# When the second group's rows are normalized and stored, and where four pieces of a column sum are added

## The reference, cut to what matters

```
def _gn(v):                       # 32 groups of one channel: mean and variance over the image
    return (v - mean) / sqrt(var + 1e-5)

x1  = x + L0(_gn(x))              # L0: 16 Fourier modes along rows, 16 along columns, plus a 1x1 mix
out = x1 + L1(_gn(x1))            # L1: deformable 3x3 convolution (offsets and mask from a 3x3 convolution)
```

## Time and profile before

| engine | busy us | share of the span |
|---|---|---|
| TensorE matmuls | 1690.6 | 95% |
| TensorE weight loads (beside matmuls) | 1326.2 | 75% |
| VectorE | 1317.5 | 74% |
| ScalarE | 1171.7 | 66% |
| GpSimd | 927.1 | 52% |

### The profile page before, as it was taken

The page is one execution under the profiler, slowest core; times in us unless marked ns, Lnnn a source line. Parts: engine busy times, 40 slices in busy tenths (PEclk is TensorE's granted clock), DMA queues, the critical chain, the costliest instruction groups (busy, mean ns, idle before and its releaser), DMA issues.

```text
span 1775.6 us, 159736 instructions
## 1 busy us (share of the span) xinstructions
PE 1690.6 (95%) x70973; PEld 1326.2 (75%) x70973; DVE 1317.5 (74%) x1964; ACT 1171.7 (66%) x1969; POOL 927.1 (52%) x1185
## 2 busy tenths in 40 slices
PE   8894579999999999999999999999999999999996
PEld 3542358888888888888888888888888888888885
DVE  7495447777777777777777777777777777777773
ACT  7175236677667676777676767776676767776773
POOL 0052335555556555655565555555565556555551
PEclk9796679999999999999999999999999999999998
DMA  9167554333333333333333333333333333333331
GB/s 383 34 252 282 178 175 123 92 85 95 99 97 84 91 99 99 86 89 97 99 89 88 90 99 96 84 92 99 98 85 90 97 99 88 88 97 99 90 89 31
DMA packets 162530, 196.58 MB, mean 111 GB/s; under 512 B 20384, under 2 KB 137536, under 8 KB 158400
## 3 DMA queue, kind: packets, MB, share of 16 engines
q1 hardware_dynamic: 162496, 196.17, 37.6%
HBM read 143.88 MB, written 52.22 MB: 110 GB/s over the span
## 4 chain that ended last, share of the span: by engine, by line
PE 91%; DMA 3%; DVE 2%; issue 1%; ACT 1%; POOL 0%; SPq 0%; DVEq 0%; POOLq 0%; ACTq 0%
PE pE L1131 18%; PE pVV L1211 16%; PE pE L1152 13%; PE pM L1177 10%; PE pVV L1152 9%; PE pVV L1165 7%; PE pR L1165 7%; PE pM L1187 4%; PE pE L1044 3%; DMA xh_scratch<-stg 1%; DMA win<-xh_scratch 1%; PE pE L1101 1%; DVE stg L846 0%; PE pVV L1079 0%; ACT stg L622 0%
## 5 line engine op out<-in xcount | busy, mean ns | idle before, releaser
L533 POOL COPY big<-win 128x480 f32<-128x480 f32 x520 | 291.7, 591 | 659.4 <-PE pVV L1165 439.6
L521 POOL TENSOR_TENSOR prod<-big 128x600 f32<-128x600 f32 (+1 forms) x489 | 499.5, 1043 | 30.0 <-POOL big L576 29.8
L666 ACT ACTIVATE big<-pE 128x768 f32<-128x768 f32 x390 | 334.3, 857 | 178.6 <-PE pE L1131 178.6
L882 DVE COPY big<-pE 128x768 f32<-128x768 f32 x390 | 373.0, 956 | 95.2 <-PE pE L1131 82.5
L888 DVE STREAM_TRANSPOSE big<-prod 128x768 f32<-128x768 f32 x390 | 377.7, 968 | 29.0 <-POOL prod L521 29.0
L1131 PE MATMUL pE<-big,sel_s 32*64 32x192 f32 x12480 | 356.9, 336 | 10.2 <-DVE big L882 7.8
L1131 PEld LDWEIGHTS pE<-big,sel_s 32*64 32x64 f32 x12480 | 219.3, 132 | 113.5 <-issue 60.7
L1211 PE MATMUL pVV<-big,wc 64*32 64x128 f32 x18720 | 293.7, 272 | 2.9 <-issue 2.0
L1211 PEld LDWEIGHTS pVV<-big,wc 64*32 64x32 f32 x18720 | 261.5, 106 | 44.4 <-issue 44.4
L1152 PE MATMUL pE<-big 60*32 60x72 f32 x20800 | 250.6, 232 | 4.5 <-issue 4.5
L1152 PEld LDWEIGHTS pE<-big 60*32 60x32 f32 x20800 | 230.6, 105 | 11.1 <-issue 5.1
(11 more groups left out here) (105 smaller groups left out, 1699.5 us busy)
## 6 DMA issues: line engine op xcount, KB each, us to landing
big<-xh_scratch SPq DMA_DIRECT2D x396, 136.0 KB
win<-xh_scratch SPq DMA_DIRECT2D x130, 408.0 KB, 3.7
xh_scratch<-stg SPq DMA_DIRECT2D x32, 544.0 KB, 2.9
big<-in_x SPq DMA_DIRECT2D x16, 1024.0 KB, 15.8
x_scratch<-big SPq DMA_DIRECT2D x16, 1024.0 KB, 4.7
x1r<-x_scratch SPq DMA_DIRECT2D x256, 64.0 KB, 3.0
out<-outs SPq DMA_DIRECT2D x256, 64.0 KB, 2.1
xh_scratch<-zero SPq DMA_DIRECT2D x4, 204.0 KB, 2.6
```

Source lines behind the costliest of these rows:

```text
L521: made = nc.gpsimd.tensor_tensor(prod[:, kx, at:at + m, 0:SQ].rearrange("p m (a b) -> p m a b", a=NSH), hy.to_broadcast(shape), hx.to_broa ...
L533: last = nc.gpsimd.tensor_copy(strips[:, half * HTP:(half + 1) * HTP, h, 0:REG].rearrange("p t (r x) -> p t r x", r=WIN_R), tiles_of(q, h, ...
L666: nc.scalar.activation(*expanded(kx, 0), ACT.Copy).then_inc(e_read, 1)
L882: nc.vector.tensor_copy(*expanded(kx, 1)).then_inc(e_read, 1)
```

## The change

Two things change. First, LATE and LATE_X1: the sixteen restores of group 1 go, one each, to the ends of VectorE's steps 1 to 16, their stores to SP's steps 2 to 17, and the eight x1 stores to SP's steps 1, 3, ..., 15. The three restores ahead of the steps are gone. The written-out part of VectorE's and SP's programs reaches to step 18 instead of 4. Second, in the first stage GpSimd adds the first two chunks of each piece of x (`pairs`, two buffers), and TensorE multiplies the other two chunks and that sum by the identity, three chunks a piece where there were four; a further semaphore (`pair_read`) tells GpSimd that a buffer has been read.

```diff
-LATE_X1 = {-3: (0,), -2: (1,), -1: (2,), 0: (3,), 1: (4,), 2: (5,), 3: (6,), 4: (7,)}
+LATE_STEPS = 16
+LATE_X1 = {2 * i + 1: (i,) for i in range(LOADS)}
-LATE = {-4: range(0, 3), -3: range(3, 6), -2: range(6, 9), -1: range(9, 12), 0: range(12, 14), 1: range(14, 16)}
+LATE = {k + 1: (k,) for k in range(LATE_STEPS)}
...
+        pairs = [big[:, HW + i * XCH:HW + (i + 1) * XCH] for i in range(2)]
...
-                peeled(at, g * NSET + 5 if apart else start)
-                at = looped(g * NSET + 5 if apart else start, (g + 1) * NSET - 3 if apart else end, g)
+                head = g * NSET + (5 if g else LATE_STEPS + 3)
+                peeled(at, head if apart else start)
+                at = looped(head if apart else start, (g + 1) * NSET - 3 if apart else end, g)
...
+            for g in range(g_count):
+                for i in range(LOADS):
+                    n = g * LOADS + i
+                    lo = i * LOADCH * XCH
+                    pool.wait_ge(x_ld[g][i], 16)
+                    if n >= 2:
+                        pool.wait_ge(pair_read, n - 1)
+                    nc.gpsimd.tensor_tensor(pairs[n % 2], X[g][:, lo:lo + XCH], X[g][:, lo + XCH:lo + 2 * XCH],
+                                            ALU.add).then_inc(pair_done, 1)
...
-            for k in LATE[-4]:
-                restore(k)
-
...
-                def add_rows(k, start, stop):
-                    return mm(pD[g][:, :], ident[:, :], X[g][:, bass.ds(k * XCH, XCH)], start=start, stop=stop)
                 for i in range(LOADS):
-                    pe.wait_ge(x_ld[g][i], 16)
-                    lo, hi = i * LOADCH, (i + 1) * LOADCH
...
-                    with pe.Fori(lo, hi) as k:
-                        add_rows(k, False, False)
-                add_rows(NXC - 1, False, True).then_inc(colsum_done, 1)
+                    n = g * LOADS + i
+                    for k in range(2, LOADCH):
+                        if k == 2:
+                            pe.wait_ge(x_ld[g][i], 16)
+                        lo = (i * LOADCH + k) * XCH
+                        mm(pD[g][:, :], ident[:, :], X[g][:, lo:lo + XCH], start=(i == 0 and k == 2), stop=False)
+                    pe.wait_ge(pair_done, n + 1)
+                    last = mm(pD[g][:, :], ident[:, :], pairs[n % 2], start=False, stop=(i == LOADS - 1))
+                    last.then_inc(pair_read, 1)
+                pe.wait_ge(pair_read, (g + 1) * LOADS)
+                pe.sem_inc(colsum_done, 1)
```

More of the change, by code:

```diff
@@ L216, in build @@
         table_done = sem("table_done")
+        pair_done = sem("pair_done")
+        pair_read = sem("pair_read")
         stg_zeroed = sem("stg_zeroed")
```

## The result

The changed kernel takes 1817.63 us (median of 4 runs, 1815.02 to 1820.21) against 1776.74 us for the kernel before on the same chips: a ratio of 1.0233, 95% interval 1.022 to 1.0245. That is 41 us slower; 1820 was forecast, in a range of 1788 to 1846. The profiled execution has a span of 1815.5 us, 39.9 more than before.

What follows compares the result with a forecast made beforehand. TensorE bounds ordinary steps and ends the column sums last; late windows behind stores delay the prologue and step 2. Sum: 1777.5 - 11.0 - 31.3 + 84.8 = 1820 us, range 1788 to 1846.

Steps and rivals of the forecast that it cites:

- The column sums: First stage: 64 chunks through TensorE become 48, VectorE is then last; the stage ends 11.0 us earlier, at least 8.
- The prologue: Before and in the first steps: without the second group's stores, loads land earlier; 23.5 us, with step 2's excess 31.3.
- My upper bound of 31: Prologue: the 23.5 us gain becomes 31 if TensorE's first pass through its loop body stalls less and the clock rises earlier.
- The sixteen steps: Steps 2 to 17: the window waits behind VectorE's restore and closes a loop; +84.8 us together, 61 to 99.
- One-store steps: Nine of steps 2 to 17, only a row store ahead of the window: 15.71 us long, +3.90 each, 35.1 us.
- two-store steps: Seven of steps 2 to 17, row store and x1 store ahead of the window: 18.91 us, +7.10 each, 49.7 us.
- the landings: Steps 2 to 17: the window lands 4.7 us after the restore's end behind one store, 7.9 behind two.
- The rest of the loop: Steps 2 to 17, from window landing to the next restore's end: 11.01 us with TensorE at half clock, 10.23 at full.
- the old excess of step 2: Step 2 took 19.56 us instead of 11.81; this 7.75 us belongs to the old stores and goes.
- A: Rival for the sixteen steps: the stores are hidden and only the gains stay, 1735 us; 6%.
- B: Rival for the sixteen steps: TensorE stays at half clock with idle time in each step, 34 us more, 1854; 13%.
- C: Rival for the first stage: column sums do not gain, VectorE's sums stretched by GpSimd or clock lost behind, 1831 us; 8%.

Runs made afterwards that it cites:

- window-first kernel: The changed kernel with the next pair's window issued ahead of the step's row store and x1 store, nothing else changed; 1733.51 us, ratio 0.9765.
- the kernel with the wait alone: Changed kernel, but in steps 2 to 17 SP waits for VectorE's restore, then issues the window, then the stores; 1772.92 us, ratio 0.9988.

## Why the prediction was right

**The column sums:** forecast -11.0, with VectorE the one who is late next. VectorE came to group 1 10.9 us earlier. At the start of the mixing matmuls 10.3 us were left; the small matmuls now start behind an idle time of 3.12 us and run slower (1.92 us for what took 1.28 before). TensorE's end at 50.2 against 50.3 forecast fits as well. What was not in the sum: alone, the sums are worth 6 us to the whole kernel, since later waits and pauses take some back; on top of the moved stores they are worth 9 (1826.39 against 1817.63).

That GpSimd would not stretch VectorE's reductions, for which I had quoted the Trainium skill ("SBUF — State Buffer", Who interferes with whom), agrees: they took 2.29 us before and 2.29 us in the kernel with the sums alone. GpSimd's own addition took 1.26 to 1.30 us, not 1.04, without consequence. Not every VectorE instruction was spared: one small addition of two inputs (at 34.45 us, beside a GpSimd addition that ended at 35.50) took 1.06 us where it had taken 0.16.

**The prologue:** measured from the first offsets matmuls, the second came 3.4 us earlier (forecast 3.4), the third 6.7 (6.8), the spread behind the first table copy 18.9 (18.6), the gather of step 0 25.9 (21.8), that of step 1 27.8 (23.5), step 2 26.2 (23.5). The gathers gained more because TensorE had full clock in stretches of steps 0 and 1 that had half clock before (the offsets matmuls there took 1.50 us each, where they had taken 2.79); the pauses took some of it away, 10.0 us against 5.1. My upper bound of 31 had counted on shorter pauses, and they got longer.

**The sixteen steps:** forecast +84.8, measured 272.4 - 189.0 = +83.4. One-store steps average 15.28 us (forecast 15.71), two-store steps 19.27 (18.91). By the chain above, windows landed at 222.32 + 6.81 = 229.13 and 241.25 + 4.38 = 245.63 us, and restores ended at 221.37, 240.78 and 255.79. So the landings were sized well: 245.63 - 240.78 = 4.85 us in step 4 (4.7) and 229.13 - 221.37 = 7.76 in step 3 (7.9); over all steps they are 4.66 to 5.13 us and 7.68 to 7.84. (The prediction's upper bound of 5.6 us for one store stood without its working.) The rest of the loop, 11.01 us for all, was not: it is 255.79 - 245.63 = 10.16 in step 4 and 240.78 - 229.13 = 11.65 in step 3, and on average 10.46 behind one store and 11.48 behind two. I had taken half clock behind every idle time, priced by one step. Behind some 3 us TensorE mostly kept full clock (the gather's first group took 1.20 us); behind 6 us it did not, and the half clock lasted longer than in the step priced (1.73 us, then 2.69 for the rest of the gather; step 2 before had 1.73, then 2.28). That these two errors, -0.55 us in nine steps and +0.47 in seven, nearly cancel is luck: with the landings they leave 1.4 us between 84.8 and 83.4. The longer written-out programs of SP and VectorE, put at nothing, show no cost: the window-first kernel has them too, and its steps take 11.7 to 12.5 us.

Sum, at step 18: -10.5 for the first stage, -26.2 for the prologue, -7.7 for the old excess of step 2, +83.4: together +39.0, of a span that grew by 39.9.

The Trainium skill ("DMA: Bandwidth & Descriptors", Queues, rings and completion order) has a semaphore write land only after the earlier writes of its DMA engine. The runs agree: with the stores behind it (the kernel with the wait alone) the window lands 3.6 to 3.9 us after its issue, with one store ahead 4.38, with two 6.81. Bytes sharing the engines would also delay it, but an x1 store issued right behind the window did not (4.52 us with it, 4.49 without). The fit of the same page of the Trainium skill (Anatomy of one DMA, stated for another queue) gave an estimated 4.2 and 6.6 us from the restore's end; 4.85 and 7.76 were measured, so the fit was low here by a seventh.

**The rivals.** A (stores hidden) needed a landing within 1.55 us of the restore's end; the shortest took 4.66. What spoke for it, hidden x1 stores in steps 3 and 4 before, holds once nothing waits: with the stores ahead of the window but no wait, one-store steps cost next to nothing, and the window-first kernel takes 1733.5 us, against the 1735 that A had named. B (half clock throughout) fell: the granted clock is 0.88 on average over the sixteen steps. C (no gain from the sums) is between: 6 of 11 us alone, 9 on top of the moved stores.

## What to carry to other kernels

A wait in the program of the engine that issues the transfers holds up everything behind it (SP stood 168.9 us in sixteen steps), so a store that waits for late work belongs behind the load that the next step needs; turning those two was worth 84 us here, and the same edit is worth 22 in the old places. Price such a move by the slack of what stands behind the wait (1.55 us from the end of the wait here, against a landing of 3.4 at best), and follow the wait round: if it comes back to the engine that ends the step, its length is added to every step. Bytes ahead of a load and a wait ahead of it do not add: 9 and 39 us alone, 84 together.

## What the runs showed of the hardware that had not been expected

- TensorE pauses at fixed places of its program in steps 0 and 1, where it runs that code for the first time: 5.1 us in all in the kernel before, 10.0 in the changed one, none while the loop repeats, and two more at its end (2.32 and 1.21 us in the changed kernel, from 1797 us on); taking 32 matmuls out of the program ahead moved a pause by 32 matmuls. All 42 pauses of steps 0 and 1 in the eleven traces end 2.2 to 3.0 us after a transfer of some 16 KB in the queue `instruction`, and so do the two at the changed kernel's end; what they wait for was not tested.
- Behind an idle time of 3.04 to 3.31 us TensorE's gather began at full clock in six of the changed kernel's one-store steps (1.20 to 1.22 us for its first group), and at half or part clock in the two with 2.37 and 3.45 us (1.73 and 1.42). In two of the six the clock fell only during the gather (step 12: granted 0.89 over the step, 16.20 us long). So the idle time alone does not decide.
- Two GpSimd additions of 512 columns for each piece of x, 32 in all and 1.28 us each, fit beside the loads and VectorE's sums without moving the end of the stage (53.03 against 53.08 us).
